# Residual by TensorE from tile 7 on, all queries on GpSimd, one scatter less in attention

## The reference

```
q = layernorm(x)                                 # per token
scaled = einsum('bsd,bse->bde', q, ctx) / 16     # 256 x 256 per sequence
attn = softmax(scaled, axis=1)                   # over d
x = x + einsum('bde,bse->bsd', attn, ctx)        # the residual x1
z = layernorm(x)
shared = silu(z @ Wg.T) * (z @ Wy.T) @ Wd.T
scores = sigmoid(z @ gate_w.T); top 2 of (scores + bias) of 8 experts
w = scores of the two, divided by their sum
out = x + shared + sum over the two experts e of w_e * (silu(z@Wg_e.T)*(z@Wu_e.T)) @ Wdown_e.T
```

## Time and profile before

| quantity | value |
|---|---|
| median of 3 runs | 221.81 us (220.78 to 221.90) |
| profiled execution, its own time | 220.29 us |
| its span, first to last instruction | 218.6 us |
| PE busy | 204.1 us (93%) |
| DVE busy | 162.8 us (75%) |
| ACT busy | 122.1 us (56%) |
| POOL busy | 115.8 us (53%) |
| mean granted TensorE clock | 0.993 |

### The profile page before, as it was taken

How to read it: one execution, slowest core, us unless ns; L and a number is a source line. 1 busy time by engine, 2 the same in 40 slices (tenths; PEclk the granted TensorE clock), 3 DMA queues, 4 the chain that set the end, 5 groups by cost and what they waited for, 6 DMA issues and landing times.

```text
span 218.6 us, 5146 instructions
## 1 busy us (share of the span) xinstructions
PE 204.1 (93%) x1349; PEld 171.6 (79%) x1349; DVE 162.8 (75%) x603; ACT 122.1 (56%) x381; POOL 115.8 (53%) x171
## 2 busy tenths in 40 slices
PE   6997899899998999999999999899999999999990
PEld 6854567576675888878789888799999999987780
DVE  3486878999988547689647679877777777765993
ACT  3498999998865322225304565565666665553200
POOL 3367878788688777777400343354455445444100
PEclk9999999999999999999999999999999999999997
DMA  5989977699221132223223335344544444593598
GB/s 149 287 284 357 309 223 260 190 283 290 87 76 49 57 112 92 105 90 114 77 78 74 104 103 150 90 137 126 150 128 147 131 144 128 152 327 131 152 382 283
DMA packets 27596, 36.12 MB, mean 165 GB/s; under 512 B 5200, under 2 KB 22352, under 8 KB 27568
## 3 DMA queue, kind: packets, MB, share of 16 engines
q1 hardware_dynamic: 24160, 26.22, 40.2%
q0 software_dynamic: 3408, 9.57, 12.0%
HBM read 22.02 MB, written 13.75 MB: 164 GB/s over the span
## 4 chain that ended last, share of the span: by engine, by line
PE 66%; DVE 14%; ACT 11%; issue 5%; POOL 2%; DVEq 0%; POOLq 0%; ACTq 0%
PE bank L1008 12%; PE bank L1009 11%; PE bank L1010 11%; PE bank L1106 7%; ACT att L600 6%; DVE nb L729 4%; PE bank L1164 4%; PE bank L1192 3%; PE bank L1128 2%; PE bank L1204 2%; PE bank L1118 2%; PE bank L1209 2%; PE bank L1208 2%; PE bank L1205 2%; PE bank L1206 2%
## 5 line engine op out<-in xcount | busy, mean ns | idle before, releaser
L560 POOL DMA_INDIRECT expert_out<-att,yi x39 | 37.6, 963 | 58.6 <-ACT att L567 58.0
L487 POOL DMA_INDIRECT slot_rows<-z_all,desti x32 | 31.9, 997 | 10.3 <-issue 10.2
L1008 PE MATMUL bank<-uph,xh 128*128 x78 | 28.6, 367 | 1.9 <-DVE xl L944 1.0
L600 ACT ACTIVATE att<-bank,nb 128x256 f32<-128x256 f32 x64 | 29.6, 493 | 0.9 <-DVE nb L729 0.9
L663 ACT ACTIVATE att<-bank 128x176 f32<-128x176 f32 x39 | 12.4, 317 | 24.2 <-PE bank L1010 24.2
L1009 PE MATMUL bank<-upl,xh 128*128 x78 | 25.3, 324 | 0.0
L1010 PE MATMUL bank<-uph,xl 128*128 x78 | 25.1, 322 | 0.0
L729 DVE TENSOR_REDUCE nb<-bank 128x2 f32<-128x512 f32 x32 | 20.5, 682 | 3.1 <-PE bank L1023 3.1
L944 DVE TENSOR_TENSOR xl<-bank,xh 128x256 fp32r<-128x256 f32 x39 | 16.5, 424 | 7.1 <-ACT xh L567 6.8
L1034 PE MATMUL bank<-att,vT 128*64 128x256 f32 x128 | 17.4, 392 | 4.4 <-POOL vT L512 4.0
L959 DVE TENSOR_TENSOR q<-att,bank 128x176 f32<-128x176 f32 x39 | 13.1, 336 | 11.3 <-ACT att L663 11.3
(11 more groups left out here) (148 smaller groups left out, 563.3 us busy)
## 6 DMA issues: line engine op xcount, KB each, us to landing
cr<-slot_rows SPq DMA_DIRECT2D x39, 136.0 KB, 2.1
upl_raw<-up_wT SPq DMA_DIRECT2D x8, 352.0 KB, 3.5
cr<-ctx_kv SPq DMA_DIRECT2D x16, 128.0 KB, 4.1
crT<-ctx_kvT SPq DMA_DIRECT2D x16, 128.0 KB, 3.4
dnl_raw<-down_wT SPq DMA_DIRECT2D x8, 256.0 KB, 4.4
z_all<-expert_out SPq DMA_DIRECT2D x4, 512.0 KB, 7.3
out<-x_all SPq DMA_DIRECT2D x7, 256.0 KB, 3.3
y_all<-expert_out SPq DMA_DIRECT2D x3, 512.0 KB, 5.7
```

What stands on the lines that cost most here:

```text
L487: nc.gpsimd.indirect_dma_start(slot_rows, bass.IndirectOffsetOnAxis(ap=desti[:, k, t:t + 1], axis=0), z_all[:, t, :], None).then_inc(sent, 16)
L560: nc.gpsimd.indirect_dma_start(expert_out, bass.IndirectOffsetOnAxis(ap=yi[:, t:t + 1], axis=0), ys[t % 3], None).then_inc(y_out[t % 3], 16)
L600: last = nc.scalar.activation(att[:, j, m:m + D], ps_s[j][b][:, c * D:(c + 1) * D], ACT.Exp, bias=nb[:, j, n:n + 1], accum_out=rs[:, j, n: ...
L1008: mm(o, ah, bh, start=(n == 0), stop=False)
```

## The change

From tile 7 on (`BY_PE = 7`), PE writes x itself into the output bank with the identity as the other operand, where the two filler matmuls stood, and `attend` accumulates on it; ACT copies the sum to `x_all` (`residual`), and DVE's `add_attention` is left out for these tiles. All 16 queries are made by POOL (`queries`, a tensor_scalar with two per-row scalars) right behind `deviations`; ACT makes none, and its `normalised` makes only z. Step 12 sends one scatter where it sent two, so 7 of the 32 go in attention and 25 after it.

```diff
+        BY_PE = 7
+        def x1_ready(k):
+            return (x1_done, k + 1) if k < BY_PE else (x1_copied, k + 1 - BY_PE)
...
-                for i in range(2 if p in (NT - 4, NT - 3, NT - 1) else 1):
+                for i in range(2 if p in (NT - 3, NT - 1) else 1):
...
+            def queries(k):
+                j = (k - 3) % 2
+                pool.wait_ge(nm_done, k + 1)
+                if k >= 2:
+                    pool.wait_ge(sc_done, B2 * (k - 1))
+                nc.gpsimd.tensor_scalar(q[:, k % 2, :], x_all[:, k, :], rstd[:, j, 1:2], nm[:, j, 1:2],
+                                        ALU.mult, ALU.add).then_inc(q_done, 1)
...
                 if live(p - 1) or live(p + 3):
                     deviations(p)
+                if live(p + 3):
+                    queries(p + 3)
...
+            def residual(k):
+                act.wait_ge(out_done, k + 1)
+                copy(x_all[:, k, :], ps_o[k % 2]).then_inc(x1_copied, 1)
...
+                if live(p - 1) and p - 1 >= BY_PE:
+                    residual(p - 1)
...
-                dve.wait_ge(x1_done, k + 1)
+                dve.wait_ge(*x1_ready(k))
...
-                if live(p - 1):
+                if live(p - 1) and p - 1 < BY_PE:
                     add_attention(p - 1)
...
-                                  start=(c == 0), stop=(c == DC - 1))
+                                  start=(c == 0 and k < BY_PE), stop=(c == DC - 1), skip_group_check=True)
...
-                        pe.wait_ge(x1_done, p - 1)
-                    keep_warm(FILL if p else WARM, p % 2)
+                        pe.wait_ge(*x1_ready(p - 2))
+                    if p < BY_PE:
+                        keep_warm(FILL if p else WARM, p % 2)
+                    else:
+                        mm(ps_o[p % 2], ident[:], x_all[:, p, :], start=True, stop=False, skip_group_check=True)
```

More of the change, by code:

```diff
@@ L192, in xattn_moe_kernel @@
         vt_done, out_done, x1_done = sem("vt_done"), sem("out_done"), sem("x1_done")
+        x1_copied = sem("x1_copied")
         z_done = sem("z_done")
@@ L603, in exponentials, with normalised @@
                 last.then_inc(exp_done, 1)
[L605 to L614, removed]
-                if live(p - 1):
-                    k = p - 1
-                    nc.scalar.activation(z_all[:, k, 0:D], x_all[:, k, :], ACT.Identity, bias=nm[:, j, 0:1],
-                                         scale=rstd[:, j, 0:1]).then_inc(z_done, 1)
+            def residual(k):
+                act.wait_ge(out_done, k + 1)
+                copy(x_all[:, k, :], ps_o[k % 2]).then_inc(x1_copied, 1)
+            def normalised(k):
+                j = (k + 1) % 2
+                act.wait_ge(nm_done, k + 5)
+                nc.scalar.activation(z_all[:, k, 0:D], x_all[:, k, :], ACT.Identity, bias=nm[:, j, 0:1],
+                                     scale=rstd[:, j, 0:1]).then_inc(z_done, 1)
             def from_z_bank(p):
@@ L634, in _ @@
                     exponentials(p, 1)
+                if live(p - 1) and p - 1 >= BY_PE:
+                    residual(p - 1)
                 if up_split(p) is not None:
                     expert_high(up_split(p), False)
-                if live(p + 2) or live(p - 2):
-                    normalised(p - 1)
+                if live(p - 2):
+                    normalised(p - 2)
                 from_z_bank(p)
@@ L1189, in _ @@
                         pe.wait_ge(hm_pad, 1)
-                        pe.wait_ge(x1_done, NT)
+                        pe.wait_ge(*x1_ready(NT - 1))
                     for c in range(DC):
```

## The result

The changed kernel takes 226.2 us (median of 4 runs, 225.4 to 227.65) against 221.3 us (220.52 to 221.9) for the kernel before on the same chip: ratio 1.023, interval 1.019 to 1.027. It is 4.9 us slower; 221.7 was forecast, with a range up to 223.4. The profiled execution took 226.38 us, its span is 224.6 us, the granted clock 0.994 as before (0.993). The two profiled executions lie 6.0 us apart in span (224.6 and 218.6), more than the medians.

The account below looks back on a forecast made before the run. ACT mostly bounds attention, and POOL would replace it at 3.77 us a step. Attention -0.5 and hand-over +0.4 give -0.1 us: profiled 220.29 becomes 220.2, and 1.5 more for the median gives 221.7 us, range 219.8 to 223.4.

Parts of the forecast that it names:

- Residual on PE at 0: Attention, PE: identity product replaces two filler products of like length (0.43 against 0.45 us), so costed at 0.
- The new wait is covered: Attention, DVE: its wait for ACT's copy of the sum hides behind two maxima, 1.29 us long.
- x = 0.44, bounds 0.31 and 0.57: POOL in attention: start-to-start time of one query, taken halfway between the 256-column memset and `vT`.
- threshold (0.55): POOL's query: from x of about 0.55 us on, the dear query decides.
- the forecast's case: Whole kernel: the prediction's main case, 221.7 us, own range 220.8 to 222.7, chance 0.40.
- A full POOL step is 3.33 + x = 3.77: Attention: POOL's step with a query, in us; POOL has no idle time in steps 2 to 10 and replaces ACT as limit.
- The 1.72: POOL in attention: us for `upl` and the start of the next operation, one term of the full POOL step.
- the sum: Whole kernel: -0.5 us for attention and +0.4 at the hand-over make -0.1 us.
- The hand-over: Attention to routed experts: slot data 0.5 us later, PE waits some 0.4 before its first slot transposes; +0.4.
- What would show it: Profile after: listed signs; forecast wrong if x leaves 0.31 to 0.57, PE never waits, or `ve` paces steps 4 to 6.
- The dear query: Rival, POOL in attention: query costs what `vT` costs, 0.57, step 3.90, attention 1.0 late; 223.2 us, chance 0.25.
- Everything behind that moves with PE: Kernel after PE reaches the routed experts: shifts along with PE, no term of its own.

Follow-up runs that it names:

- e2: Kernel before with only the residual on PE and the copy on ACT from tile 7, queries left with ACT, eight scatters: 221.34 us, ratio 1.001.
- e5: Changed kernel with `neg` and `ve` as tensor_reduce over one input each: ratio 1.012 (1.003 to 1.021).
- e7: Kernel before with `neg` and `ve` as tensor_reduce: four runs, 226.63 to 230.9 us, too far apart for a ratio.
- e14: Kernel before with `neg` and `ve` as tensor_reduce, once more: 221.13 us, ratio 1.001 (0.998 to 1.005).
- e4: Changed kernel with `neg` alone written as a tensor_reduce: 226.97 us, ratio 1.022 (1.012 to 1.031).
- e17: Changed kernel with a memset of 256 columns on POOL behind each `upl` in steps 4 to 10: ratio 1.028 (1.022 to 1.034).
- e3: Kernel before with only the scatter table changed, seven scatters in attention: 221.02 us, ratio 0.997 (0.994 to 1.0005).
- e11: Kernel before with residual by PE and ACT from tile 7, `neg` and `ve` as tensor_reduce, queries on ACT, eight scatters: 221.23 us, ratio 1.002.
- e12: Changed kernel itself, unchanged, run again in a later batch: 225.79 us, ratio 1.021 (1.015 to 1.026) to the kernel before.
- e13: Changed kernel with `neg` and `ve` as tensor_reduce, once more: 224.16 us, ratio 1.013 (1.0075 to 1.018).
- e1: Kernel before with only the queries changed, all made on POOL: 226.04 us, ratio 1.017 (1.008 to 1.026).
- e16: Kernel before with residual by PE and ACT from tile 7, `neg` and `ve` as tensor_reduce, eight scatters, queries 6, 8, 10, 12 on POOL: ratio 0.996.
- e18: Same as e16, run once more in another batch: ratio 0.993 (0.988 to 0.998) to the kernel before.

## Why the prediction was wrong

*Residual on PE at 0: right.* e2 has +0.2 us in all (-0.3 to 0.9).

*The new wait is covered: right.* Among DVE's waits in the changed kernel there is none for ACT's copy into `x_all`, and e2 loses nothing by it. ACT ceased to be the limit, as said.

*x = 0.44, bounds 0.31 and 0.57: too low.* It is 0.52 start to start (34.59 to 35.11), and `nm` to the query is 0.30, not 0.27. Together that is 0.11 us per step. By the prediction's own threshold (0.55) this was still the forecast's case.

*A full POOL step is 3.33 + x = 3.77: this is the step that failed.* It is 4.10. Of the 0.33 missed, 0.11 is the line above; 0.22 is the distance from `upl` to the next `rstd`, put at 1.72 and measured at 1.94. (The 1.72 is slightly high itself: without the wait gives 1.69, and e5 measures 1.64.) The prediction read the 0.28 of waiting for `ve` in the earlier trace rows as DVE's own lateness, which POOL's longer queue would swallow. For the kernel before that reading was correct (e7, e14). What it left out is that DVE, once it is early, can't do `neg` while `upl` runs: it is early only until it hits POOL's operation. e4 shows the hold passing from `neg` to `ve`, e5 shows the step at 3.80 without it. The SBUF page of the Trainium skill ("SBUF — State Buffer", section Who interferes with whom) describes this: VectorE and GpSimd share one pair of ports as an exclusive lock; `tensor_scalar` and instructions with two SBUF inputs can run into it, `tensor_reduce` never does. The rows agree on all three: `neg` 0.92 as tensor_scalar and 0.16 as a reduction, `ve` 0.77 with two inputs and 0.15 as a reduction. It also says that a VectorE instruction with two SBUF inputs contends with a GpSimd instruction that reads SBUF, not with one that only writes it. e17's memset only writes, and `neg` and `ve` both ended with it; since `ve` stands behind `neg`, these rows don't tell which of the two it held.

*From there the sum follows, as far as attention's end.* `vT` of tile 2 came at 18.75, forecast 18.9; tile 0 was 0.30 late in the profile where 0.56 was forecast, but profiles differ there by more than that. Six steps at 4.13 on average instead of 3.77 make 2.2 us; less the 0.15 from the start that is 43.53 instead of 41.5 for tile 8. Two more steps and `place` add 0.8 (tile 10 at 52.29 instead of 49.5). From tile 10 to attention's end the changed kernel gains 0.4 on the kernel before (20.40 and 20.79 us); 0.7 was forecast. So attention ends 2.61 late where 0.5 early was forecast: 3.1 us of the miss.

*The hand-over: right in size.* A wait of 0.4 before the first transposes was forecast; 0.42 is there, and 0.44 in e3 alone. The price is 3.16 - 2.61 = 0.55 us.

*What would show it:* "DVE's `ve`, not POOL, still sets the pace in steps 4 to 6" was named as the thing that would make the forecast wrong. It is what the trace shows, [0.26 <-DVE ve] in each of these steps, though by way of POOL.

*The rivals.* The dear query (223.2) took the right side and the right size of x, but it too had a POOL step without the wait: 3.90. None had the ring closed.

*Behind the hand-over: a second step that failed, and still open.* "Everything behind that moves with PE" put the rest of the kernel at nothing. The first slot transposes are 3.16 us late and the medians 4.9 apart, so some 1.7 us come later. The profiles, 6.0 us apart in span, show 1.0 of it in the slots (the last scatter of results starts at 206.13 and 201.96, 4.17 late) and 1.8 in the last loads and stores (18.5 us from that scatter to the end of the span, 16.6 before). In the slots PE waits once for a late slot load:

```profile
178.61 0.20 PEld L1185 LDWEIGHTS bank<-ident,cr 128*128 128x128 f32 x2 [0.30 <-DMA cr<-slot_rows]
...
179.61 0.42 PE L1025 MATMUL bank<-uph,xh 128*128 x1 [0.56 <-issue]
```

The next scatter is 1.13 late for it. The same gap of 1.0 to 1.1 us stands at the same slot in e2, e4, e11, e12 and e13, and not in the kernel before. But e2 and e11 are no slower in all than the kernel before, so it can't simply be counted as loss. In the last loads and stores the changed kernel, e4, e12 and e13 have 18.5 to 19.4 us, the kernel before, e1, e2, e3 and e11 16.6 to 17.9. e13 shows how much is unexplained: its attention ends level with the kernel before's (70.05), its transposes are 0.55 late, and its total is 3.1 us above. What makes the load and the end late wasn't tried.

## What to carry to other kernels

Before work is moved to GpSimd, look at what VectorE does while GpSimd's long operations run: a tiny VectorE operation of the wrong form can wait for the long one to end (0.92 us instead of 0.17 here), and if GpSimd waits for that operation's result, the two serialize. In the trace it is a row of 128x2 that takes longer than its like and ends with the other engine's row. And before a wait is written off as slack, work out when the waited-for engine could have come at the earliest, and what would hold it then; a load that fits neither of two full engines may fit when it alternates between them (e16 and e18 gained 0.4 and 0.7%).

## What the runs showed of the hardware

- A `tensor_scalar` of 2 columns on DVE: 0.17 us free, 0.92 while a two-input operation of 704 columns runs on POOL, 1.30 for one (`sul`) that it met earlier, 1.36 with a memset behind it. A `tensor_reduce` of as many columns took 0.15 to 0.16 in the same place (e5, e13), a two-input operation 0.77 (e4).
- On POOL a `tensor_scalar` of 256 columns with two per-row scalars is 0.52 us from start to start, nearly what a product of two inputs costs (0.57): half the inputs saved a tenth. The memset of 256 columns, 0.31, was no guide.
- With the first queries on ACT `vT` of tile 2 comes at 17.3 to 18.5 us, with a query on POOL ahead of each of the first `vT` at 18.7 to 19.9: so the start is later there, by 1 us or more in most of them.
